# One residual subtraction per half block split in two by PSUM bank, with signals per bank, in a graph network layer on Trainium2

## What is computed

```python
h = relu(layernorm(x))                                  # no scale and shift
agg = segment_sum(edge_attr, src, num_segments=50000)   # row per node
z = concatenate([h, agg], axis=-1)                      # 256 wide
z = silu(z @ W1 + b1) @ W2 + b2                         # 256 -> 256 -> 128
out = x + layernorm(z) * gamma + beta + h
```

## Time and profile before

| | us |
|---|---|
| median of 3 timed runs | 728.91 (728.89 to 729.11) |
| span of the profiled execution | 769.9 |
| PE busy | 711.9 |
| DVE busy | 713.3 |
| ACT busy | 629.7 |
| POOL busy | 490.1 |

### The profile page before, as it was taken

How to read it: one execution, slowest core, us unless ns; L and a number is a source line. 1 busy time by engine, 2 the same in 40 slices (tenths; PEclk the granted TensorE clock), 3 DMA queues, 4 the chain that set the end, 5 groups by cost and what they waited for, 6 DMA issues and landing times.

```text
span 769.9 us, 15386 instructions
## 1 busy us (share of the span) xinstructions
PE 711.9 (92%) x4554; PEld 592.7 (77%) x4554; DVE 713.3 (93%) x2275; ACT 629.7 (82%) x2034; POOL 490.1 (64%) x414
## 2 busy tenths in 40 slices
PE   7999998689999999999999999999999999999994
PEld 3555546578888888888888888888888888888883
DVE  8999997889999999999999999999999999999888
ACT  7999985478878787878787888787879788879793
POOL 3000017577878777778777777777777777777730
PEclk9999999799999999999999999999999999999997
DMA  5000000123333333333333333333323233322112
GB/s 203 1 2 1 2 3 23 46 76 105 104 103 105 104 104 103 106 105 103 105 105 101 104 102 105 103 105 102 107 100 112 96 107 102 108 90 81 49 65 78
DMA packets 28265, 65.89 MB, mean 86 GB/s; under 512 B 8473, under 2 KB 10028, under 8 KB 28180
## 3 DMA queue, kind: packets, MB, share of 16 engines
q1 hardware_dynamic: 15604, 51.90, 18.6%
q0 software_dynamic: 12576, 12.99, 7.0%
HBM read 52.05 MB, written 25.60 MB: 101 GB/s over the span
## 4 chain that ended last, share of the span: by engine, by line
DVE 43%; PE 22%; issue 20%; another core or an unknown queue 6%; ACT 6%; DVEq 0%
DVE stat L824 9%; DVE R L1031 7%; DVE R L1006 6%; PE za L702 6%; DVE lo L1024 5%; DVE T L1036 4%; PE y L658 4%; ACT hi L549 4%; PE za L653 2%; PE pre L653 2%; PE za L646 2%; PE za L687 2%; PE pre L646 2%; DVE guess_off L879 1%
## 5 line engine op out<-in xcount | busy, mean ns | idle before, releaser
L436 POOL DMA_INDIRECT G<-in_edge_attr_dram,slot_edge x388 | 479.9, 1237 | 144.0 <-issue 123.2
L741 PEld LDWEIGHTS y<-w2c,S 128*128 128x128 f32 (+1 forms) x1556 | 189.9, 193 | 9.4 <-issue 1.4
L741 PE MATMUL y<-w2c,S 128*128 128x128 f32 (+1 forms) x1556 | 191.0, 276 | 1.3 <-ACT S L556 1.3
L539 ACT ACTIVATE H<-X,shift,rstd 128x128 f32<-128x128 f32 x392 | 163.4, 508 | 2.7 <-issue 2.7
L716 PE MATMUL pre<-hi,w1h 128*128 128x512 f32 (+1 forms) x392 | 163.4, 417 | 1.9 <-issue 1.2
L1024 DVE TENSOR_TENSOR lo<-za,hi 128x1024 fp32r<-128x1024 f32 (+1 forms) x98 | 119.4, 1218 | 42.3 <-ACT hi L549 35.7
L717 PE MATMUL pre<-hi,w1l 128*128 128x512 f32 (+1 forms) x392 | 154.6, 394 | 0.0
L556 ACT ACTIVATE S<-pre,b1c 128x512 f32<-128x512 f32 (+1 forms) x196 | 127.4, 723 | 8.2 <-remote 4.7
L721 PE MATMUL pre<-lo,w1h 128*128 128x512 f32 (+1 forms) x392 | 122.8, 394 | 0.1
L824 DVE BATCH_NORM_STATS2 stat<-X 128x6 f32<-128x128 f32 x392 | 107.6, 285 | 0.1
L702 PE MATMUL za<-HOT,G 128*128 128x128 f32 (+1 forms) x784 | 105.1, 277 | 2.3 <-issue 1.6
(11 more groups left out here) (154 smaller groups left out, 990.3 us busy)
## 6 DMA issues: line engine op xcount, KB each, us to landing
X<-in_x_dram SPq DMA_DIRECT2D x48, 512.0 KB
out_dram<-R SPq DMA_DIRECT2D x48, 512.0 KB
G<-in_edge_attr_dram,slot_edge POOLq DMA_INDIRECT x388
X<-in_x_dram SPq DMA_DIRECT2D x1, 424.0 KB
out_dram<-R SPq DMA_DIRECT2D x2, 192.0 KB
w1f<-in_L_gnn_W_dram SPq DMA_DIRECT2D x1, 256.0 KB, 2.7
w2f<-in_L_gnn_W_dram SPq DMA_DIRECT2D x1, 128.0 KB, 2.7
srci<-in_src_dram SPq DMA_DIRECT2D x1, 85.8 KB
```

Source lines behind the costliest of these rows:

```text
L436: nc.gpsimd.indirect_dma_start(G[b.j][:, t, :], None, source, bass.IndirectOffsetOnAxis(ap=slot_edge[:, bass.ds(b.number(TILES, t), 1)], a ...
L539: done = nc.scalar.activation(H0[b.j][:, t, :], X[b.xj][:, t, :], ACT.Relu, bias=shift[b.j][:, t:t + 1], scale=rstd[b.ring(POWERS_LAG)][:, ...
L741: done = nc.tensor.matmul(places[t][0:r], S[c][:, m, t * r:(t + 1) * r], w2c[:, m, :], start=False, stop=True, skip_group_check=True)
```

## The change

`hi_done` now goes up after each of the two casts, twice a half. `split_low` becomes two subtractions of 512 columns, one for each bank, each waiting for the cast of its bank, and `lo_done` goes up after each. `turn_h` waits for the first `hi` and `lo` operation of the half before (those that read bank 0); `sum_edges` gets waits of its own for the second ones (bank 1). `layer1` waits for both casts, and for each `lo` operation before the product that reads it. The two waits of POOL's `pace` on `lo_done` count in the new units and wait for the second operation.

```diff
 def pace(b, c, k):
-    at_least(pool, lo_done, b.half(1, 1, 1))            # c == 0 and k == 0
+    at_least(pool, lo_done, b.half(1, 2, 2))
...
-    at_least(pool, lo_done, b.plus(1).half(0, 1, 1))    # c == 0 and k == 3
+    at_least(pool, lo_done, b.plus(1).half(0, 2, 2))
...
 def split_high(b, c):
-    nc.scalar.copy(hi[c][:, 0, w], za[:, 0, w])
+    nc.scalar.copy(hi[c][:, 0, w], za[:, 0, w]).then_inc(hi_done, 1)
     act.wait_ge(agg_done, b.half(c, 1, 1))
     nc.scalar.copy(hi[c][:, 1, w], za[:, 1, w]).then_inc(hi_done, 1)
...
 def turn_h(b, c):
     pe.wait_ge(h0_done, b.half(c, 1, 1))
-    at_least(pe, hi_done, b.half(c))
-    at_least(pe, lo_done, b.half(c))
+    at_least(pe, hi_done, b.half(c, 2, -1))
+    at_least(pe, lo_done, b.half(c, 2, -1))
...
 def sum_edges(b, c):
     pe.wait_ge(hot_done, b.number(1, 1))
+    at_least(pe, hi_done, b.half(c, 2, 0))
+    at_least(pe, lo_done, b.half(c, 2, 0))
...
 def layer1(b, c):
-    pe.wait_ge(hi_done, b.half(c, 1, 1))
+    pe.wait_ge(hi_done, b.half(c, 2, 2))
...
-        if m == 0:
-            pe.wait_ge(lo_done, b.half(c, 1, 1))
         for k in range(2):
+            if m == 0:
+                pe.wait_ge(lo_done, b.half(c, 2, k + 1))
             done = nc.tensor.matmul(pre[m][:, w], w1h[:, k, cols], lo[c][:, k, w], start=False, stop=(k == 1))
...
 def split_low(b, c):
-    dve.wait_ge(hi_done, b.half(c, 1, 1))
     at_least(dve, pre_done, b.half(c, 2, -2))
     w = slice(0, HALF * rows_of(b))
-    nc.vector.tensor_tensor(out=lo[c][:, :, w], in0=za[:, :, w], in1=hi[c][:, :, w].bitcast(F32),
-                            op=ALU.subtract).then_inc(lo_done, 1)
+    for k in range(2):
+        dve.wait_ge(hi_done, b.half(c, 2, k + 1))
+        nc.vector.tensor_tensor(out=lo[c][:, k, w], in0=za[:, k, w], in1=hi[c][:, k, w].bitcast(F32),
+                                op=ALU.subtract).then_inc(lo_done, 1)
```

## The result

The changed kernel takes 734.43 us (median of 4 runs, 734.24 to 734.66) against 729.01 of the kernel before on the same chip: a ratio of 1.0075 (95% interval 1.0063 to 1.0087). The forecast was 734.0. The profiled execution has a span of 732.5 us, where 740 had been forecast and the trace of before showed 769.9. Of the 64 timed executions of the kernel before in this study, 63 lie between 728.57 and 729.69 us; one took 1818.72, has no trace, and is left out of the ratios.

The account below looks back on a forecast made before the run. The prediction took the timed kernel to be bound by DVE alone: 728.9 + 6.9 for the split - 1.8 at the ends, signals and earlier starts 0, gave 734.0 us; likeliest case 731.8 to 737, whole range 719 to 742.

Parts of the forecast that it names:

- The timed kernel is bound by DVE: Timed runs: DVE alone sets the pace, needing 12.06 us a block against PE's 11.90.
- The step that took 41.0 us out of DVE's idle time: Span 769.9 against median 728.9: 41.0 off DVE's 56.6 idle leaves 15.6, some 1.3 of it before lo.
- the ring binds the timed runs: Rival: the lo, transposes, sums, casts cycle limits timed runs as in the profile; 699 to 705 us, chance 0.10.
- half and half: Rival: shorter DVE instructions explain part of 41.0 us; 10 to 20 us of lo waits vanish; 716 to 726, chance 0.12.
- late signals of PE are something recording adds: ACT's casts starting 1.39 and 2.38 us after PE's modelled ends in dense stretches may come from recording.
- DVE's idle sum against the gap to the median: DVE's 56.6 us idle less the 41.0 gap between span and timed median bounds waits before lo at 15.6.
- The price of the split: DVE's lo: 98 more operations at a fixed 0.07 us each, +6.9 us, bounds 5.9 and 12.7.
- Earlier transposes and sums are worth nothing: PE's transposes start 0.53 us earlier, sums 0.40, but the gain meets slack in timed runs and is worth 0.
- the slack of 0.53: Second cast ends 3.96 us after lo's start, DVE reaches the next lo at 4.49: 0.53 us to spare.
- -1.8 us at three places of 0.6: Ramp and near the end: only half the subtraction follows the second cast, 3 x 0.6 us gained, bounds 0 and -3.
- Signals and pacing cost nothing: Extra increments on ACT and DVE, PE's extra waits and POOL's gathers 0.07 us later: taken as 0.
- The margin to PE: PE's 11.90 us a block is only 0.16 under DVE's 12.06.

Follow-up runs that it names:

- e1: The kernel before, unchanged, profiled once more: 728.94 us, ratio 0.9999, span 727.0.
- e2: The kernel before with only the subtraction split in two, both after both casts, signals and waits as before: 735.83 us, 1.0094.
- e4: The changed kernel with four subtractions of 256 columns, two for each bank: 745.84 us, 1.0232 against the kernel before.
- e7: The changed kernel's signals, subtraction split only in the first two and last two blocks, elsewhere one operation: 730.07 us, 1.0011 against the kernel before.
- e6: The changed kernel with the residual left out on seven of eight tiles, so less DVE work: 719.29 us, 0.9863 against the kernel before.
- e5: The kernel before with the residual left out on seven of eight tiles, so less DVE work: 720.05 us, 0.9875.
- e3: The changed kernel's signals and waits, but one 1024-column subtraction after both casts raising lo_done by two: 730.96 us, 1.0027 against the kernel before.
- e12: The kernel before with both R additions moved into the small chain's gaps, POOL's third gather waiting for the second scaling instead: 751.63 us, 1.0314.
- e8: The kernel before with DVE reordered: R additions into places 7 and 0, one-hots ahead of lo, statistics one place on: 722.34 us, 0.9907.

## Why the prediction was right, and where it was wrong

**The timed kernel is bound by DVE: right, and the reason given for it half wrong.** The step that took 41.0 us out of DVE's idle time held: e1 has 3.3 us idle before `lo`, where 1.3 to 15.6 had been derived, and DVE is busy for 710.0 us there against 713.3. That also answers the rivals "the ring binds the timed runs" and "half and half": they needed DVE's own work to be up to 41 us shorter, and it is 3.3 shorter. The explanation beside it, that late signals of PE are something recording adds, fell: e1 and the changed kernel are recorded the same way, and their spans lie 1.6 and 1.9 us under the times of the same executions. From it followed one wrong number, the changed kernel's span: 740 forecast (from 769.9), 732.5 measured. The rule "DVE's idle sum against the gap to the median" worked without knowing why the trace was slow. That 1.3 came so near 3.3 is in part luck: a time exceeds its span by some 1.9 us, so that the gap was 42.9 and not 41.0, and by it nothing would have been left.

**The price of the split: 98 x 0.07 = 6.9 us forecast, 6.7 measured (e2).** The distances agree: 0.60 from one 512-column operation to the next, for the additions of rows 8 and for the changed kernel's `lo` ((382.06 - 380.86) / 2). Averaged over the steady part, the operation behind `lo` starts 1.135 us after it in e1 and 1.202 in the changed kernel. In durations the split would look dearer, about 0.15 us (2 x 0.682 - 1.213, the mean of one): the durations overlap, and what a full engine pays is the distance. The Trainium skill ("VectorE: DVE Perf Modes", the section on the TRN2 errata) has 120 cycles for a PSUM source, by which, as an estimate from that page, 98 operations would have been 12.3 us. That is near the part seen in durations, and not what the split cost here, 0.069 us each in e2 and 0.058 in e4.

**Earlier transposes and sums are worth nothing: right, and by a shorter way than reckoned.** The transposes come 0.83 us after `lo`'s start where e2 has 1.43 (averages of the steady part), but the casts don't follow: the second starts 3.36 after `lo` in the changed kernel, 3.35 in e2 and 3.29 in e1. In front of them on ACT stands the copy of the bias (L578), which waits for DVE's T (`[1.61 <-DVE T L1039]`), and T has not moved forward. The gain of 0.53 is lost there and never meets the slack of 0.53 that the prediction set against it. That slack is there too: the second cast is ready 0.52 us before DVE in the changed kernel and 0.53 in e1. A block takes 12.13 us in the changed kernel and in e2, without any of the new signals.

**-1.8 us at three places of 0.6: about the right size, at other places than thought.** The changed kernel is 1.4 us under e2 in the medians and 0.9 in the spans (733.4 against 732.5); e7 gave 1.6 gross. One of the places is the first `lo` of all. In e2, with the second place where it waits:

```profile
121.14 1.29 DVE L1025 TENSOR_TENSOR lo<-za,hi 128x512 fp32r<-128x512 f32 x2 [1.28 <-ACT hi L549]
122.34 1.25 DVE L824 BATCH_NORM_STATS2 stat<-X 128x6 f32<-128x128 f32 x6
133.20 1.29 DVE L1025 TENSOR_TENSOR lo<-za,hi 128x512 fp32r<-128x512 f32 x2 [1.16 <-ACT hi L549]
```

In the changed kernel:

```profile
120.05 0.69 DVE L1027 TENSOR_TENSOR lo<-za,hi 128x512 fp32r<-128x512 f32 x1 [0.18 <-ACT hi L547]
121.16 0.69 DVE L1027 TENSOR_TENSOR lo<-za,hi 128x512 fp32r<-128x512 f32 x1 [0.41 <-ACT hi L549]
121.77 1.64 DVE L826 BATCH_NORM_STATS2 stat<-X 128x6 f32<-128x128 f32 x8
132.58 1.38 DVE L1027 TENSOR_TENSOR lo<-za,hi 128x512 fp32r<-128x512 f32 x2 [1.16 <-ACT hi L547]
```

At the first place the work behind starts at 121.77 instead of 122.34, 0.57 earlier: the 0.6 forecast for a place. The second gives nothing, since DVE waits as long (1.16) for the first cast there as e2 does for the second. The rest comes in the last block, before whose second `lo` the lead over e2 grows from 0.38 us (702.16 against 702.54) to 0.94 (712.11 against 713.05). The waits from which the three places were read, 6.6 us put to "issue" in 2 places, were of the odd trace: e1 has none put to "issue" and 3.2 us before `lo` in 3 places. That the term came out near is therefore in part luck.

**Signals and pacing cost nothing: right for the change** (e6 against e5), with e3's 1.9 us of its own beside it.

**The margin to PE: 0.16 us a block forecast, 0.15 measured (e1 to e5).** The number is right by some luck: PE's 11.90 is one half of 5.95 doubled, and the other half of rows 6 takes 407.79 - 401.28 - 0.43 = 6.08, with which PE's block would be 12.03 and the margin 0.03. The rival "the ring binds the timed runs", 699 to 705, was a true mechanism at the wrong place: in e12 it takes 1.1 us less cover for the ring to bind.

## What to carry to other kernels

Before explaining a profile, hold its span against the timed median: where the span is 40 us longer, the waits in it may be those of another execution, and the idle time that the gap leaves over bounds what can be won. Where two engines are full, the chain of waits doesn't tell which one is the bound; a little work added to one of them does. Before counting an earlier signal as a gain, look at what stands in front of the work that it releases: here a copy that waited for something else took the whole gain. On an engine that is busy 98%, splitting an operation to signal earlier costs its fixed part each time and earns only where somebody waits; here each split was 0.06 to 0.07 us and hardly anybody waited. What helped was work for the gaps that were there: 7.0 us (e8). When work is moved, look at every engine that is paced by its signal, not only at the data: the same move cost 133 us through a gather's pacing.

## What the runs showed of the hardware that was not expected

One execution of an unchanged program took a span of 769.9 us where others take 727.0, with the same mean granted clock (0.99), slower gathers (1237 against 1155 ns) and casts that began up to 2.8 us after both ACT was free and the product was there, where the others took at most 0.04. It is the only one of these 14 traces that looks so. Its cause is open.

Two operations of 512 columns in a row start 0.60 us apart and last 0.68 each: a row of operations costs less than the sum of its durations.
